# Attention and FFN layer: eight up tiles with one scale group's products in a PSUM bank of their own

## The chip, the cores and the metric

One core of one Trainium2 chip runs the kernel. The metric is the device time of one execution in microseconds. TensorE does the matrix products (PE in the profile), VectorE (DVE), ScalarE (ACT) and GpSimd (POOL) do the rest, and the SP queue issues the transfers.

## The reference

Sixteen sequences of 512 rows by 512 columns pass one transformer layer. The attention has 16 heads, low-rank queries and keys, ALiBi distances and a causal mask. The feed-forward part has 4-bit weights with one scale for each 128 inputs of an output row; that is the part which the change touches.

```python
x = x + _layernorm(attn(_layernorm(x), Wq_down, Wq_up, Wkv_down, k_up, v_up, Wo))
x = x + _layernorm(ffn(_layernorm(x), gate_up_packed, gate_up_scales, down_packed, down_scales))

def ffn(x, ...):                       # I = 1408, GROUP_SIZE = 128, H = 512: four groups of inputs
    w_gu = codes(gate_up_packed) * repeat(gate_up_scales.T, 128)      # [2816, 512]
    w_down = codes(down_packed) * repeat(down_scales.T, 128)          # [512, 1408]
    gate, up = split(x @ w_gu.T)
    y = (silu(gate) * up) @ w_down.T
    return y / sqrt(mean(y * y) + 1e-6)
```

## The kernel before, in words

The kernel works through 17 steps. Step t does the attention of sequence t and, beside it, the feed-forward part of sequence t - 1. Step 0 has attention alone, step 16 the feed-forward part alone, steps 1 to 15 have both. Every engine has its own written-out list of instructions, and semaphores tie the lists together; no scheduler moves anything.

**Precision.** fp32 values go through TensorE as a high and a low fp16 half, so one product of 128 inputs needs three matmuls of 128x512: high by high, high by low, low by high. A gate or up tile is 128 of the 1408 outputs for all 512 rows of a sequence. It sums four groups of inputs. The weights of such a tile are divided by the scale of the last group, so that the last group's weights are bare 4-bit codes, exact in fp16, and need two matmuls. That makes 3 x 4 - 1 = 11 matmuls (`GU_PRODUCTS`) for each of the 22 tiles (gate and up of m = 0 to 10). A down tile takes 33 matmuls, and there are four. Together 374 matmuls for each sequence.

**Slots.** The attention of a step is cut into 64 slots (`SLOTS`). Slots 0 to 22 compute the row maxima of two tiles each (`maximum` on TensorE, L1133 on VectorE, `row_sum` on ScalarE); slots 23 to 40 one such tile and one tile of exponentials; slots 41 to 63 two tiles of exponentials each. In slots 0 to 22 an even slot has tiles 128 and 256 wide in banks low0 and low1, an odd one 384 and 512 wide in score0 and score1. The exponentials of four heads are masked by GpSimd (`keep_causal(s)`, in the slot of e = 4s + 5) and multiplied into psO (`values(s)`, TensorE, in the slot of e = 4s + 7). After the maxima of its slot, TensorE runs a share of the 374 matmuls, from `cut(slot)` to `cut(slot + 1)`, by the weights in `PER_SLOT`; the first 22 run ahead of slot 0.

**The feed-forward jobs.** Job numbers run gate 0, up 0, gate 1, up 1 and so on, and take the three banks dense0 to dense2 in turn: a job may open only when the job three before it has been released (`open_job`). So up(m) opens when gate(m - 1) has been released, and gate(m + 2) when up(m) has. `up_done(m, up)` is the slot in which TensorE finishes the tile. One slot later ScalarE runs `tanh(m)`; two slots later VectorE runs `gate(m)` (L944), which releases the gate's bank. Two slots after the up tile is finished, VectorE runs `up(m)` (L952), which multiplies the bank into `tb` and releases it, and `h_high(m)` (L967); GpSimd follows with `h_low(m)` (L1260). All of these stand behind the maxima of their slot in the engine's list.

**The output rows.** Down tile i is copied by ScalarE (`y_copy(i)`, slot `down_done(i) + 1`), measured by VectorE (`y_moments(i)`, + 2), its root taken by GpSimd (`power(t, "lo", ...)`, L1190, + 3), normalised by VectorE (`y_norm(i)`, + 4) and added to the input by GpSimd (`y_add(i)`, L1266, + 5). The statistics of the next sequence (`ln1`) run on VectorE in slot 43 (`LN1_SLOT`, L828), their power on GpSimd in slot 45 (`LN1_POWER`) and the normalisation in slots 46 to 49. GpSimd's list decides: in slot 45 it waits first for the statistics of ln1, then for those of y 0, and only then does `keep_causal(6)`.

Of the kernel before, what the change touches and what calls it, by code (L numbers as in the profile page):

```python
# [65 lines left out]
LN1_SLOT, LN1_POWER, LN1_NORM = 43, 45, 46  # L66
# [20 lines left out]
LIFT = 8  # L87
D_PRODUCTS = 3 * MI
# [7 lines left out]
UP_PRODUCTS = 2 * MI * GU_PRODUCTS  # L96
# [24 lines left out]
def up_done(m, up):  # L121

    return done(GU_PRODUCTS * (2 * m + up + 1))
# [7 lines left out]
def layer_program(nc, x, wq_down, wq_up_t, wkv_down_t, k_up_t, v_up_t, wo_t, gu_packed, gu_scales,  # L131
# [6 lines left out]
    with ctx:  # L138
# [73 lines left out]
        h_scale = sb("h_scale", [P, MI], f32)  # L212
        st6 = {n: sb("st6_" + n, [P, NT, 6], f32) for n in ("ln1", "ln2", "ln3", "lo")}
# [19 lines left out]
        def st_bank(e):  # L233

            return score[e % 2] if e < THREE else (score + low_bank[1:])[e % 3]

# [122 lines left out]
        def _(pe):  # L359
# [49 lines left out]
            def step(t, att, ffn, nxt):  # L409
# [73 lines left out]
                def ffn_up(m, up, a, b):  # L483
# [5 lines left out]
                    tt = terms(lambda s, c: wgu[:, KC * s + c, col:col + P], lambda s, c: x2t[:, s, c, :], KC - 1)  # L489
                    tt += [(wgu[:, KC - 1, col:col + P], x2t[:, s, KC - 1, :]) for s in range(2)]  # L490
                    for c in range(KC if m == 0 and not up else 0):
# [3 lines left out]
                    if m or up:  # L495
                        ins = products(bank(t, n)[:, :], tt[a:b], a == 0, b == GU_PRODUCTS)
                    if b == GU_PRODUCTS:
                        ins.then_inc(sem["dense"], 1)
# [13 lines left out]
                def run(a, b):  # L512

                    start = 0
                    for q in range(2 * MI):
                        lo, hi = max(a, start), min(b, start + GU_PRODUCTS)
                        if lo < hi:
                            ffn_up(q // 2, q % 2, lo - start, hi - start)
                        start += GU_PRODUCTS
# [7 lines left out]
                def lse_rows(part):  # L527

                    dst = (psO, low_bank[0])[part]
                    pe.wait_ge(sem["mh"], val("mh", t, part + 1))  # L530
# [42 lines left out]
                def values(s):  # L573
# [3 lines left out]

                    pe.wait_ge(sem["keep"], val("keep", t, s + 1))
# [56 lines left out]
        def _(act):  # L635
# [15 lines left out]
            def step(t, att, ffn, nxt):  # L651
# [22 lines left out]

                def o_copy(g):
# [40 lines left out]
                if isinstance(t, int) and t == 1:  # L716
                    act.wait_ge(s_norm, 19)
# [45 lines left out]
                if ffn:  # L763
                    tanh(0)
                for slot, (low_tiles, exp_tiles) in enumerate(SLOTS):
# [17 lines left out]
                    if ffn:  # L783
                        for m in range(MI):
                            if m and slot == max(0, up_done(m, 0) + 1):
                                tanh(m)
                    for part in range(2):
# [20 lines left out]
        def _(dve):  # L808
# [103 lines left out]
            def step(t, att, ffn, nxt):  # L912
# [34 lines left out]
                def up(m):  # L947

                    n = job_f(t, m, 1)
                    dve.wait_ge(sem["dense"], val("dense", t, n + 1))  # L950
                    taken(dve, t, job_f(t, m, 0))
                    nc.vector.scalar_tensor_tensor(tb[:, m % 2, :], tb[:, m % 2, :], h_scale[:, m:m + 1],  # L952
                                                   bank(t, n)[:, :], ALU.mult, ALU.mult).then_inc(sem["freev"], 1)

                def h_high(m):

                    taken(dve, t, job_f(t, m, 1))
# [70 lines left out]
                def y_norm(i):  # L1028

                    dve.wait_ge(sem["rs"], val("rs", t, n_y[0] + i + 1))  # L1030
# [81 lines left out]
                n_y = [3 if nxt else 2]  # L1112
# [15 lines left out]
                for slot, (low_tiles, exp_tiles) in enumerate(SLOTS):  # L1128
# [31 lines left out]
                    if nxt and slot == LN1_SLOT:  # L1160
# [4 lines left out]
                        n_ln1 = n_ve[0]  # L1165
                    if nxt and LN1_NORM <= slot < LN1_NORM + NT:
                        i = slot - LN1_NORM
                        dve.wait_ge(sem["rs"], val("rs", t, n_ln1))
# [17 lines left out]
        def _(pool):  # L1186
# [20 lines left out]
            def divisors():  # L1207
# [3 lines left out]
                def put(ins, settle=True):  # L1211
                    n[0] += 1
                    ins.then_inc(s_norm, 1)
                    if settle:
# [24 lines left out]
                                            ALU.mult), False)  # L1239
                put(nc.gpsimd.tensor_scalar(gate_scale[:, :], divisor[:, 0:MI], 0.5 / (S_X * S_GU), None, ALU.mult))  # L1240
# [4 lines left out]
            def step(t, att, ffn, nxt):  # L1245
# [5 lines left out]
                n_y = (2 if ffn else 0) + (1 if nxt else 0)  # L1251
# [256 lines left out]
```

## Time and profile before

| | before |
|---|---|
| median of 3 runs | 2429.0 us (2428.91 to 2429.45) |
| profiled execution: time, span | 2428.72 us, 2427.0 us |
| TensorE matmul busy | 2349.2 us, 97% |
| VectorE busy | 1555.9 us, 64% |
| ScalarE busy | 1400.2 us, 58% |
| GpSimd busy | 669.0 us, 28% |
| mean granted TensorE clock | 0.987 |
| chain that ended last | PE 90%, DVE 5%, ACT 2% |

The chain names, for every stretch of time, the instruction that the end of the program waited on; PE 90% says that it runs through TensorE nearly all the time. A step with both parts repeats every 144.8 us. The step that is read below has slot 0 at 464.99 us, slot 23 at 509.1 us and slot 41 at 535.4 us; the one before it has slot 41 at 390.6 us.

### The profile page before, as it was taken

What the parts mean: (1) busy time and instruction counts of PE and PEld (TensorE: products, weight loads), DVE (VectorE), ACT (ScalarE), POOL (GpSimd) and SP (SyncE); (2) the same over time, 40 slices, a digit from 0 to 9 for tenths busy, and PEclk for the clock granted to TensorE, in tenths of its full rate; (3) what the DMA queues carried; (4) which work ended last, traced back from release to release, by engine and by line L of the source; (5) the groups of instructions that cost most, each with busy time, mean ns of one, the idle gap of its engine ahead of it and who ended that gap; (6) DMA issues with size and microseconds to landing.
All of it is one profiled execution on the core that took longest, in us unless ns stands there. A gap on an engine that the chain in (4) does not pass through costs nothing.

```text
span 2427.0 us, 38384 instructions
## 1 busy us (share of the span) xinstructions
PE 2349.2 (97%) x13020; PEld 1081.5 (45%) x13020; DVE 1555.9 (64%) x4344; ACT 1400.2 (58%) x3866; POOL 669.0 (28%) x923
## 2 busy tenths in 40 slices
PE   7699999999999999999999999999999999999988
PEld 3344444444444444444444444444444444444433
DVE  7867575665757666575765757566675765757542
ACT  4757466474656647466564755647475564756610
POOL 5522223132231312223132232312323132232312
PEclk8799999999999999999999999999999999999999
DMA  5020121202112120121202012120121202012000
GB/s 151 19 65 24 36 53 36 70 19 59 30 53 53 36 70 19 38 51 45 61 20 72 17 53 53 37 70 19 45 45 45 61 28 70 18 45 53 19 18 18
DMA packets 99523, 108.89 MB, mean 45 GB/s; under 512 B 22895, under 2 KB 73199, under 8 KB 99311
## 3 DMA queue, kind: packets, MB, share of 16 engines
q1 hardware_dynamic: 98462, 105.65, 16.5%
q8 instruction: 103, 1.69, 0.3%
q10 hardware_dynamic: 864, 0.79, 0.1%
q14 instruction: 94, 0.77, 0.1%
HBM read 38.49 MB, written 16.78 MB: 23 GB/s over the span
## 4 chain that ended last, share of the span: by engine, by line
PE 90%; DVE 5%; ACT 2%; issue 1%; POOL 1%; DMA 0%; SPq 0%; POOLq 0%; DVEq 0%; ACTq 0%
PE dense L379 65%; PE psO L583 6%; PE psO L379 4%; PE score L567 4%; PE low L550 3%; PE score L550 3%; DVE st_ln L828 1%; PE low L567 1%; ACT arena L770 1%; PE low L385 1%; PE low L474 1%; PE score L474 1%; PE score L385 1%; POOL arena L1323 0%; ACT score L687 0%
## 5 line engine op out<-in xcount | busy, mean ns | idle before, releaser
L379 PE MATMUL dense<-arena,wgu 128*128 128x512 f16 x3872 | 920.2, 379 | 1.5 <-DVE arena L931 1.2
L379 PEld LDWEIGHTS dense<-arena,wgu 128*128 128x128 f16 x3872 | 369.7, 97 | 394.0 <-issue 7.7
L379 PE MATMUL dense<-wdn,arena 128*128 128x512 f16 x2112 | 533.7, 379 | 2.6 <-POOL arena L1260 2.6
L1260 POOL TENSOR_TENSOR arena<-late,arena 128x512 f16<-128x512 f32 x176 | 203.4, 1155 | 821.6 <-DVE arena L967 611.9
L1133 DVE CUSTOM_DVE_ANT_0 low<-low,mmax 128x128 f32<-128x128 f32 (+3 forms) x672 | 278.9, 436 | 226.5 <-PE low L550 223.1
L770 ACT ACTIVATE arena<-score 128x512 f32<-128x512 f32 (+3 forms) x720 | 300.4, 437 | 173.6 <-PE score L567 131.2
L687 ACT ACTIVATE low<-low,ncol 128x128 f32<-128x128 f32 (+3 forms) x672 | 299.8, 446 | 121.9 <-DVE ncol L1133 114.7
L687 ACT ACTIVATE score<-score,ncol 128x384 f32<-128x384 f32 x352 | 214.3, 609 | 141.6 <-DVE ncol L1133 141.3
L379 PEld LDWEIGHTS dense<-wdn,arena 128*128 128x128 f16 x2112 | 198.7, 98 | 183.8 <-issue 9.3
L1133 DVE CUSTOM_DVE_ANT_0 score<-score,mmax 128x384 f32<-128x384 f32 x352 | 214.0, 649 | 75.1 <-PE score L550 74.6
L1323 POOL TENSOR_SCALAR_AFFINE_SELECT arena<-arena 128x512 f32<-128x512 f32 x240 | 162.3, 676 | 292.6 <-ACT arena L770 292.6
L567 PE MATMUL score<-qst,kst 128*128 128x512 f16 (+3 forms) x784 | 218.2, 305 | 2.7 <-ACT arena L770 2.5
L583 PE MATMUL psO<-arena 128*32 128x512 f32 (+3 forms) x1920 | 177.9, 443 | 24.1 <-POOL arena L1323 22.4
L972 DVE TENSOR_SCALAR arena<-oc 128x512 f16<-128x512 f32 x64 | 27.6, 431 | 224.6 <-ACT oc L681 222.1
L550 PE MATMUL low<-kst,qst 125*128 125x128 f16 (+3 forms) x672 | 155.5, 278 | 7.7 <-ACT low L687 7.4
L770 ACT ACTIVATE arena<-low 128x384 f32<-128x384 f32 (+3 forms) x240 | 103.5, 431 | 99.1 <-PE low L567 97.1
L672 ACT ACTIVATE late<-dense,gate_scale 128x512 f32<-128x512 f32 x176 | 119.6, 680 | 58.7 <-PE dense L379 38.3
L944 DVE SCALAR_TENSOR_TENSOR late<-late,dense 128x512 f32<-128x512 f32 x176 | 120.5, 685 | 51.4 <-ACT late L672 51.4
L952 DVE SCALAR_TENSOR_TENSOR late<-late,h_scale,dense 128x512 f32<-128x512 f32 x176 | 130.9, 744 | 24.7 <-PE dense L379 24.6
L1133 DVE DVE_READ_ACCUMULATOR2_ANT ncol<- 128x1 f32 x1024 | 145.3, 142 | 0.2
L1190 POOL TENSOR_TENSOR rs_ln<-ve_ln,half 128x4 f32<-128x4 f32 x48 | 49.3, 1026 | 328.2 <-DVE ve_ln L937 323.1
L687 ACT ACTIVATION_READ_ACCUMULATOR low<-low,ncol 128x1 f32 x672 | 132.1, 197 | 0.0
(181 smaller groups left out, 2917.5 us busy)
## 6 DMA issues: line engine op xcount, KB each, us to landing
qst<-arena SPq DMA_DIRECT2D x384, 64.0 KB, 2.0
kst<-arena SPq DMA_DIRECT2D x186, 128.0 KB, 2.6
xin<-x SPq DMA_DIRECT2D x16, 1024.0 KB, 5.1
late<-x SPq DMA_DIRECT2D x64, 256.0 KB, 2.8
out<-late SPq DMA_DIRECT2D x64, 256.0 KB, 2.0
qst<-mrow SPq DMA_DIRECT2D x96, 8.0 KB, 1.9
wgu<-wo_t SPq DMA_DIRECT2D x1, 1024.0 KB, 13.1
wgu<-wq_down SPq DMA_DIRECT2D x1, 768.0 KB, 4.4
```

The costliest lines, as they stand in the source:

```text
L379: ins = nc.tensor.matmul(dst, w, a, start=first and k == 0, stop=last and k == len(tt) - 1)
L550: nc.tensor.matmul(mx_bank(k)[:, 0:P * (i + 1)], qst[0:P - 3, h, P * i:P * i + P], kst[0:P - 3, h, 0:P * (i + 1)], start=True, stop=True). ...
L567: ins = nc.tensor.matmul(st_bank(e)[:, 0:wide], kst[:, h, P * kt:P * kt + P], qst[:, h, P * kt:L], start=True, stop=h >= STEEP)
L583: ins = nc.tensor.matmul(psO[HD * a:HD * a + HD, P * kt:L], v[:, kt, HD * (HG * g + a):HD * (HG * g + a) + HD], prob_of(s)[:, a, 0:wide], ...
L672: nc.scalar.activation(tb[:, m % 2, :], bank(t, n)[:, :], ACT.Tanh, scale=gate_scale[:, m:m + 1]).then_inc(sem["tanh"], 1)
L687: nc.scalar.activation(mx_bank(k)[:, 0:wide], mx_bank(k)[:, 0:wide], ACT.Exp, scale=-1.0, bias=ncol[:, k:k + 1], accum_out=scol[:, k:k + 1 ...
L770: nc.scalar.activation(prob_of(e // HG)[:, e % HG, 0:wide], st_bank(e)[:, 0:wide], ACT.Exp, scale=1.0 / S_SCORE).then_inc(sem["exp"], 1)
L944: nc.vector.scalar_tensor_tensor(tb[:, m % 2, :], tb[:, m % 2, :], 1.0, bank(t, n)[:, :], ALU.add, ALU.mult).then_inc(sem["freev"], 1)
L952: nc.vector.scalar_tensor_tensor(tb[:, m % 2, :], tb[:, m % 2, :], h_scale[:, m:m + 1], bank(t, n)[:, :], ALU.mult, ALU.mult).then_inc(sem ...
L1133: nc.vector.tensor_tensor_reduce(out=mx_bank(k)[:, 0:wide], in0=mx_bank(k)[:, 0:wide], in1=mmax[:, L - wide:L], scale=-1.0 / S_SCORE, scal ...
L1260: nc.gpsimd.tensor_tensor(ht[:, 1, m, :], tb[:, m % 2, :], ht[:, 0, m, :], ALU.subtract).then_inc(sem["hl"], 1)
L1323: nc.gpsimd.affine_select(out=diagonal, in_=diagonal, compare_op=ALU.is_ge, fill=0.0, base=0, pattern=[[0, HG], [1, P]], channel_multiplie ...
```

## The change

One more matmul can be saved in a tile if the third group (columns KC - 2) is also stored as bare codes: its product, two matmuls instead of three, then has another scale than the other groups and must be summed in a bank of its own. This is done for the up tiles m = 0, 1, 2, 3, 4, 5, 8, 9 (`BARE`), in steps 1 to 16. For these tiles:

- TensorE runs 8 matmuls into the main bank and 2 into psO (in step 16 into score0 or score1), 10 in place of 11. The first of the two waits for the previous copy out of psO (semaphore `bare`).
- ScalarE has a new instruction `bare_copy(m)`, one slot after the tile is finished: psO, times `bare_scale`, into the SBUF tile `own`.
- VectorE's `up(m)` becomes two instructions: an addition of the main bank and `own`, which releases the main bank and first waits for `bare`; then the multiplication by `tb`, from SBUF, which raises the new semaphore `whole`. `h_high(m)` waits for `whole`.

The sequence then has 366 matmuls, and `cut` deals these out over the same slots, so tiles begin and end at other places. The slots of `up_done(m, 0)` for m = 5, 6, 9, 10 go from 13, 16, 25, 30 to 12, 15, 24, 29, those of `up_done(m, 1)` for m = 7, 8, 10 from 20, 23, 32 to 19, 22, 31, and `down_done(1)` from 47 to 46. `LN1_SLOT`, `LN1_POWER` and `LN1_NORM` go from 43, 45, 46 to 45, 47, 48, with the counts of `rs` and `ve` to match. In step 0 GpSimd has three more small instructions.

```diff
-LN1_SLOT, LN1_POWER, LN1_NORM = 43, 45, 46
+LN1_SLOT, LN1_POWER, LN1_NORM = 45, 47, 48
...
+BARE = (0, 1, 2, 3, 4, 5, 8, 9)
+BARE_LOGS = 6
+def gu_products(q):
+    return GU_PRODUCTS - 1 if q % 2 and q // 2 in BARE else GU_PRODUCTS
...
+        def bare_bank(t, m):
+            return score[m % 2] if isinstance(t, int) and t == B else psO
...
+                    own_tt = [(wgu[:, KC - 2, col:col + P], x2t[:, s, KC - 2, :]) for s in range(2)] if bare else []
...
+                    if bare and b > last - n_own:
+                        first = max(a - (last - n_own), 0)
+                        if first == 0:
+                            k = BARE.index(m)
+                            if att and k == 0:
+                                taken(pe, t, j["V"] + 2)
+                            if att and k == BARE_LOGS:
+                                pe.wait_ge(sem["mrowc"], val("mrowc", t, 1))
+                            if k > (0 if att else 1):
+                                pe.wait_ge(sem["bare"], val("bare", t, k if att else k - 1))
+                        ins = products(bare_bank(t, m)[:, :], own_tt[first:b - (last - n_own)], first == 0, b == last)
...
+                def bare_copy(m):
+                    k = BARE.index(m)
+                    act.wait_ge(sem["dense"], val("dense", t, job_f(t, m, 1) + 1))
+                    if k:
+                        act.wait_ge(sem["whole"], val("whole", t, k))
+                    nc.scalar.activation(own[:, :], bare_bank(t, m)[:, :], ACT.Copy,
+                                         scale=bare_scale[:, m:m + 1]).then_inc(sem["bare"], 1)
...
+                            if m and m in BARE and slot == up_done(m, 1) + 1:
+                                bare_copy(m)
...
+                    values_ = bank(t, n)[:, :]
+                    if m in BARE:
+                        k = BARE.index(m) + 1
+                        dve.wait_ge(sem["bare"], val("bare", t, k))
+                        nc.vector.scalar_tensor_tensor(own[:, :], values_, 1.0, own[:, :], ALU.mult, ALU.add
+                                                       ).then_inc(sem["freev"], 1)
+                        taken(dve, t, job_f(t, m, 1))
+                        values_ = own[:, :]
                     taken(dve, t, job_f(t, m, 0))
                     nc.vector.scalar_tensor_tensor(tb[:, m % 2, :], tb[:, m % 2, :], h_scale[:, m:m + 1],
-                                                   bank(t, n)[:, :], ALU.mult, ALU.mult).then_inc(sem["freev"], 1)
+                                                   values_, ALU.mult, ALU.mult
+                                                   ).then_inc(sem["whole" if m in BARE else "freev"], 1)
```

Where the three engines stand now is shown by the order of their instructions. First VectorE in slots 4 and 5 of a step: the maxima (L1133, after L1205), `up(1)` and `h_high(1)`. Before:

```order
L1133 ISA low1,ncol<-low1,mmax 128x256 [waits s_mx]
L1133 ISA ncol 128x1
L952 SCALAR_TENSOR_TENSOR late<-late,h_scale,dense1 128x512 [waits s_freev,s_dense]
L967 TENSOR_SCALAR arena<-late 128x512 [waits s_freev]
L1133 ISA score0,ncol<-score0,mmax 128x384 [waits s_mx]
```

After:

```order
L1205 ISA low1,ncol<-low1,mmax 128x256 [waits s_mx]
L1205 ISA ncol 128x1
L1016 SCALAR_TENSOR_TENSOR own<-dense1,own 128x512 [waits s_bare,s_dense]
L1021 SCALAR_TENSOR_TENSOR late<-late,h_scale,own 128x512 [waits s_freev]
L1040 TENSOR_SCALAR arena<-late 128x512 [waits s_whole]
L1205 ISA score0,ncol<-score0,mmax 128x384 [waits s_mx]
```

The addition with its wait for ScalarE's copy stands between the maxima of slot 4 and those of slot 5.

TensorE in slot 7, where `up(3)` opens bank dense2, which `gate(2)` releases. Before:

```order
L550 MATMUL score0<-kst,qst 128x384 [waits s_rowsum]
L550 MATMUL score1<-kst,qst 128x512 [waits s_rowsum]
L379 MATMUL dense1<-arena,wgu 128x512 x3
L379 MATMUL dense2<-arena,wgu 128x512 [waits s_freev]
L379 MATMUL dense2<-arena,wgu 128x512 x3
```

After:

```order
L595 MATMUL score0<-kst,qst 128x384 [waits s_rowsum]
L595 MATMUL score1<-kst,qst 128x512 [waits s_rowsum]
L404 MATMUL dense1<-arena,wgu 128x512
L404 MATMUL dense2<-arena,wgu 128x512 [waits s_freev]
L404 MATMUL dense2<-arena,wgu 128x512 x5
```

The wait for the release has moved up by two matmuls within the slot. In the same way `gate(8)`, which opened as the second matmul of slot 20, now opens as the last of slot 19, while the up tile that it waits for is still read in VectorE's slot 19.

GpSimd in slots 36 to 50 (`keep_causal` is L1323 before and L1398 after; the group of four is 2 to 5). Before:

```order
L1323 AFFINE_SELECT arena<-arena 128x4x128 [waits s_exp] x4
L1190 TENSOR_TENSOR rs_ln<-ve_ln,half 128x4 [waits s_ve]
L1190 TENSOR_TENSOR rs_lo<-ve_lo,half 128x1 [waits s_ve]
L1323 AFFINE_SELECT arena<-arena 128x4x128 [waits s_exp]
L1266 TENSOR_TENSOR late<-late 128x512 [waits s_yn]
L1323 AFFINE_SELECT arena<-arena 128x4x128 [waits s_exp] x2
```

After:

```order
L1398 AFFINE_SELECT arena<-arena 128x4x128 [waits s_exp] x4
L1261 TENSOR_TENSOR rs_lo<-ve_lo,half 128x1 [waits s_ve]
L1398 AFFINE_SELECT arena<-arena 128x4x128 [waits s_exp]
L1261 TENSOR_TENSOR rs_ln<-ve_ln,half 128x4 [waits s_ve]
L1341 TENSOR_TENSOR late<-late 128x512 [waits s_yn]
L1398 AFFINE_SELECT arena<-arena 128x4x128 [waits s_exp]
```

The power of ln1 now stands behind `keep_causal(6)` instead of ahead of it. Further on `y_add(1)` (slot 51 in place of 52) has moved ahead of `keep_causal(9)`, which stands in slot 52.

## Rows read from the trace of the kernel before

**Rows 1.** The page: busy time, share of the span and instructions of each engine.

```profile
PE 2349.2 (97%) x13020; PEld 1081.5 (45%) x13020; DVE 1555.9 (64%) x4344; ACT 1400.2 (58%) x3866; POOL 669.0 (28%) x923
```

**Rows 2.** Stretches: busy us (instructions) of PE, PEld, DVE, ACT, POOL; slots 0-22, step.

```profile
464.99:509.10 44.11, 44.11 (x223) 21.02 (x222) 34.36 (x114) 31.05 (x102) 12.32 (x23) 1.00 0.12 27
...
428.10:573.00 144.90, 143.72 (x809) 65.89 (x806) 94.08 (x267) 86.79 (x241) 38.25 (x54) 1.00 0.17 45
```

**Rows 3.** Waits of PE: us in total, times, longest; the whole run, then one step.

```profile
PE psO L583 <- POOL arena L1323: 22.4, 16, 5.3
```

```profile
PE psO L583 <- POOL arena L1323: 1.2, 1, 1.2
```

**Rows 4.** Timeline of PE, slots 4 to 7 and 19: start, us, line, operation, tiles.

```profile
472.73 1.67 PE L379 MATMUL dense<-arena,wgu 128*128 128x512 f16 x7
474.24 0.54 PE L550 MATMUL score<-kst,qst 125*128 125x384 f16 x2
...
476.14 0.33 PE L550 MATMUL low<-kst,qst 125*128 125x128 f16 x2
...
478.03 0.54 PE L550 MATMUL score<-kst,qst 125*128 125x384 f16 x2
...
501.49 0.54 PE L550 MATMUL score<-kst,qst 125*128 125x384 f16 x2
```

**Rows 5.** Timeline of DVE: up(1), h_high(1), slot 5, gate(2), later up(6).

```profile
473.57 0.74 DVE L952 SCALAR_TENSOR_TENSOR late<-late,h_scale,dense 128x512 f32<-128x512 f32 x1
474.35 0.43 DVE L967 TENSOR_SCALAR arena<-late 128x512 f16<-128x512 f32 x1
474.76 0.57 DVE L1133 CUSTOM_DVE_ANT_0 score<-score,mmax 128x384 f32<-128x384 f32 x1
...
477.46 0.69 DVE L944 SCALAR_TENSOR_TENSOR late<-late,dense 128x512 f32<-128x512 f32 x1 [0.17 <-ACT late L672]
...
503.14 0.74 DVE L952 SCALAR_TENSOR_TENSOR late<-late,h_scale,dense 128x512 f32<-128x512 f32 x1
```

**Rows 6.** Timeline of ACT: last row sums of slots 3 and 5, then tanh(2).

```profile
472.28 0.66 ACT L687 ACTIVATE score<-score,ncol 128x512 f32<-128x512 f32 x1
...
476.07 0.66 ACT L687 ACTIVATE score<-score,ncol 128x512 f32<-128x512 f32 x1
...
476.75 0.68 ACT L672 ACTIVATE late<-dense,gate_scale 128x512 f32<-128x512 f32 x1
```

**Rows 7.** DVE timeline: a three-operand instruction from SBUF; ACT group: a plain copy from PSUM.

```profile
444.35 2.73 DVE L1055 SCALAR_TENSOR_TENSOR late<-arena,rs_ln,late 128x512 f32<-128x512 f32 x4
```

```profile
L708 ACT ACTIVATE late<-dense 128x512 f32<-128x512 f32 x64 | 39.4, 615 | 84.0 <-PE dense L379 84.0
```

**Rows 8.** Slots 43 to 52, one step earlier: timelines of DVE, POOL and PE.

```profile
396.67 2.47 DVE L828 BATCH_NORM_STATS2 st_ln<-xin 128x6 f32<-128x512 f32 x4
```

```profile
399.95 1.04 POOL L1190 TENSOR_TENSOR rs_ln<-ve_ln,half 128x4 f32<-128x4 f32 x1 [2.71 <-DVE ve_ln L937]
401.44 0.55 POOL L1190 TENSOR_TENSOR rs_lo<-ve_lo,half 128x1 f32<-128x1 f32 x1 [0.45 <-DVE ve_lo L1026]
...
403.27 1.50 POOL L1266 TENSOR_TENSOR late<-late 128x512 f32<-128x512 f32 x1 [0.68 <-DVE late L1035]
404.72 0.83 POOL L1323 TENSOR_SCALAR_AFFINE_SELECT arena<-arena 128x512 f32<-128x512 f32 x1
...
410.14 1.27 POOL L1266 TENSOR_TENSOR late<-late 128x512 f32<-128x512 f32 x1 [0.68 <-DVE late L1035]
411.37 0.63 POOL L1323 TENSOR_SCALAR_AFFINE_SELECT arena<-arena 128x512 f32<-128x512 f32 x1
```

```profile
402.64 0.64 PE L583 MATMUL psO<-arena 128*32 128x256 f32 x8 [1.18 <-POOL arena L1323]
...
405.69 0.43 PE L583 MATMUL psO<-arena 128*32 128x128 f32 x8
...
411.15 0.85 PE L583 MATMUL psO<-arena 128*32 128x384 f32 x8
```

More of the change, by code:

```diff
@@ L65, with norm_of_y, norm_of_x @@
 LN2 = 0.6931471805599453
-LN1_SLOT, LN1_POWER, LN1_NORM = 43, 45, 46
+LN1_SLOT, LN1_POWER, LN1_NORM = 45, 47, 48
+def norm_of_y(i, nxt):
+    return i + (4 if nxt and i else 3)
+def norm_of_x(ffn):
+    return 4 if ffn else 1
 BEHIND = 4
@@ L95 @@
 PER_SLOT[17], PER_SLOT[18], PER_SLOT[41] = 11, 10, 11
-UP_PRODUCTS = 2 * MI * GU_PRODUCTS
+UP_PRODUCTS = sum(gu_products(q) for q in range(2 * MI))
 ALL_PRODUCTS = UP_PRODUCTS + NT * D_PRODUCTS
@@ L121, in up_done @@
 def up_done(m, up):
-    return done(GU_PRODUCTS * (2 * m + up + 1))
+    return done(sum(gu_products(q) for q in range(2 * m + up + 1)))
 def down_done(i):
@@ L212, in layer_program @@
         h_scale = sb("h_scale", [P, MI], f32)
+        bare_scale = sb("bare_scale", [P, MI], f32)
+        own = sb("own", [P, L], f32)
         st6 = {n: sb("st6_" + n, [P, NT, 6], f32) for n in ("ln1", "ln2", "ln3", "lo")}
@@ L488, in ffn_up @@
                     col = I * up + P * m
-                    tt = terms(lambda s, c: wgu[:, KC * s + c, col:col + P], lambda s, c: x2t[:, s, c, :], KC - 1)
+                    last = gu_products(2 * m + up)
+                    bare = up and m in BARE
+                    tt = terms(lambda s, c: wgu[:, KC * s + c, col:col + P], lambda s, c: x2t[:, s, c, :],
+                               KC - 2 if bare else KC - 1)
                     tt += [(wgu[:, KC - 1, col:col + P], x2t[:, s, KC - 1, :]) for s in range(2)]
+                    own_tt = [(wgu[:, KC - 2, col:col + P], x2t[:, s, KC - 2, :]) for s in range(2)] if bare else []
+                    n_own = len(own_tt)
                     for c in range(KC if m == 0 and not up else 0):
@@ L529, in lse_rows @@
                     dst = (psO, low_bank[0])[part]
+                    if ffn and part == 0:
+                        pe.wait_ge(sem["bare"], val("bare", t, BARE_LOGS))
                     pe.wait_ge(sem["mh"], val("mh", t, part + 1))
@@ L576, in values @@
                     wide = L - P * kt
+                    if s == 0 and ffn:
+                        pe.wait_ge(sem["bare"], val("bare", t, len(BARE)))
                     pe.wait_ge(sem["keep"], val("keep", t, s + 1))
@@ L764, in step @@
                     tanh(0)
+                    bare_copy(0)
                 for slot, (low_tiles, exp_tiles) in enumerate(SLOTS):
@@ L1239, in divisors @@
                                             ALU.mult), False)
+                pool.wait_ge(s_norm, n[0])
+                put(nc.gpsimd.tensor_scalar(bare_scale[:, :], scales[:, MI:2 * MI, GROUPS - 2], 1 / (FP8_SCALE * S_GU), None,
+                                            ALU.mult))
+                for lo, hi in ((0, 6), (8, 10)):
+                    put(nc.gpsimd.memset(scales[:, MI + lo:MI + hi, GROUPS - 2], FP8_SCALE * S_GU), False)
                 put(nc.gpsimd.tensor_scalar(gate_scale[:, :], divisor[:, 0:MI], 0.5 / (S_X * S_GU), None, ALU.mult))
@@ L1329, in step @@
                     for i in range(NT):
-                        power(t, "lo", n_y + i + 1, i, i + 1)
+                        power(t, "lo", norm_of_y(i, nxt), i, i + 1)
                         y_add(i)
@@ L1344, in step @@
                     if nxt and slot == LN1_POWER:
-                        power(t, "ln1", n_y)
+                        power(t, "ln1", norm_of_x(ffn))
                     if isinstance(t, int) and t == 0:
```

36 lines of the change are left out of this document (19 added, 17 removed), and 2 rows, old and new, of the table COUNTS.

## The prediction, made before the changed kernel ran

> **What bounds the kernel now.** I read the page first, then the stretches, then the waits of TensorE. TensorE is busy for 97% of the span [rows 1], and in slots 0 to 22 of a step it has no gap at all: 44.11 us busy in 44.11 [rows 2]. In a whole step of 144.9 us it is idle for 1.2 us [rows 2, 3], at one place, `values(6)` in slot 47. So a matmul fewer is worth its own time, if nobody else is late next. Who could be late is the second thing to read. In slots 0 to 22 VectorE is busy for 34.4 of 44.1 us (78%) and ScalarE for 31.1 (70%) [rows 2], far more than their means of 64% and 58% [rows 1]. Six of the eight changed tiles lie there.
>
> **Matmuls removed.** Seven matmuls take 1.51 us (the first starts at 472.73, the next row-maximum at 474.24) [rows 4], 0.216 us each. A step with eight changed tiles saves 8 x 0.216 = 1.73 us of TensorE time, 16 steps save 27.6 us.
>
> **Work added.** VectorE: an addition of the form of `gate` (bank and SBUF, 0.69 us) and the multiplication, now from SBUF, at (2.73 - 0.69) / 3 = 0.68 us [rows 5, 7]. Between two dependent instructions there are 0.04 us (473.57 + 0.74, next at 474.35) [rows 5]. ScalarE: one copy with a pointer scale; the nearest rows are a plain copy at 0.615 and tanh, with a pointer scale, at 0.68 [rows 6, 7]. I take 0.66, near the tanh row. Its time alone lies beside TensorE's; its order does not.
>
> **What the order costs: a walk through one unit.** Slot 3, ScalarE: the last row sum starts at 472.28, and 0.68 later (as 476.07 to 476.75) the engine is free [rows 6], so `bare_copy(1)` runs from 472.96 to 473.62. Slot 4, VectorE: `up(1)`, which began at 473.57, now begins at 473.66 with the addition; 0.73 on comes the multiplication, 0.72 on `h_high`, and 0.41 on (474.35 to 474.76) slot 5's maxima: 475.52 instead of 474.76 [rows 5], 0.77 late. The row sums of slot 5, then tanh(2), then `gate(2)` each wait for the one before, so `gate(2)` ends at 477.46 + 0.69 + 0.77 = 478.92. TensorE opens `up(3)` behind that release. It used to do so after three matmuls of slot 7; now slot 7 starts 0.22 earlier (one matmul less in slots 0 to 6) and `up(3)` opens after one: 478.03 - 0.22 + 0.38 (an odd slot's two maxima) + 0.22 = 478.41. The release with 0.04 for the semaphore is at 478.96: TensorE **waits 0.55 us**.
>
> I carried the three lists on through slots 7 to 22 with durations read as start to start in the timelines of rows 4 to 6 (even slot: VectorE 0.60, ScalarE 0.38 + 0.47; odd slot: 1.13 and 0.64 + 0.68; gate 0.65, changed up tile 1.8 to 1.9, tanh and copy 0.57 and 0.55 until the next starts). With the old order they give the rows of slots 3 to 6 back to 0.02 us. One pass from the start of slot 5's maxima to those of slot 8's is 1.31 (to the second row maximum's value) + 0.68 + 0.72 (tanh) + 0.65 + 1.13 + 1.80 = 6.29 us, the next, through an even slot and `bare_copy`, 5.71; the mean is 6.0. TensorE needs for a unit of gate and up, 21 matmuls and 2.9 slots' maxima, 4.53 + 0.80 = 5.33. So the loop VectorE-ScalarE-VectorE becomes slower than TensorE for five units. In us from the start of slot 0, release against opening: up(3) 13.98 against 13.43, up(4) 19.53 against 19.23, up(5) 25.98 against 24.99. Waits: 0.55 + 0.30 + 0.99. The openings behind an addition, gate(3) to gate(7), come out with 0.5 to 1.1 us in hand, because it is the addition that releases.
>
> A fourth wait has nothing to do with lateness. `gate(8)` now opens as the last matmul of slot 19 and needs `up(6)`, which VectorE does in slot 19. Slot 19 started at 501.49 and `up(6)` was done at 503.14 + 0.74 = 503.88, 2.39 after the slot began [rows 4, 5]; TensorE gets there 0.38 + 6 x 0.216 = 1.68 after. Wait: 0.75. Sum of slots 0 to 22: **2.6 us a step**, for 15 steps. In slots 23 to 40 the same walk gives about 0.2 us, at row sums.
>
> The Trainium skill ("VectorE: DVE Perf Modes", section on the TRN2 errata) puts a ScalarE instruction from PSUM at 172 cycles plus one for each column, at 1.2 GHz; as an estimate that is 0.57 us for 512 columns. The rows have 0.615 for the plain copy [rows 7]. With 0.57 in place of 0.66 the three late releases would come about 0.1 us earlier each, and the total 4 us lower.
>
> **Slots 41 to 53.** Before, GpSimd takes the power of y 0 at 401.44, because VectorE does the four statistics of ln1 (from 396.67) first; `keep_causal(6)` stands behind it, and TensorE waits 1.18 us at 402.64 [rows 8]. With ln1 two slots later that wait goes, in 14 steps. What is late next: `keep_causal(7)` now stands behind ln1's power and `y_add(0)`. VectorE: y 0 from 396.9 for 1.49 (401.44 - 399.95), ln1 3.12 (from 396.75 to 399.87), so the power starts at 401.6 and takes 1.04, `y_add(0)` 1.27 to 1.50, `keep_causal(7)` 0.63 to 0.83 [rows 8]: done at 404.5 to 405.0. TensorE wants it at 405.69 - 1.18 - 0.22 = 404.29. Wait 0.2 to 0.7, I take 0.4. Then `y_add(1)` has moved ahead of `keep_causal(9)`. It starts at 410.14, tied to the copy after `values(7)`, and the mask behind it ran from 411.37 to 412.00; `values(9)` is wanted at 411.15 - 0.22 = 410.93 [rows 8]. Wait 1.1 us, in 15 steps, as the other sequence's statistics play no part in it.
>
> **The sum.** Steps 1 to 14: -1.73 - 1.18 + 2.6 + 0.2 + 0.4 + 1.1 = +1.4, x 14 = +19.5. Step 15, without ln1: -1.73 + 2.6 + 0.2 + 1.1 = +2.2. Step 16: the copy hides between tiles that are 4.5 us apart, -1.73. Step 0: its one wait of 5.3 us at the same `values` [rows 3] may go wholly or be replaced, 0 to -5.3; VectorE and GpSimd carry work on the weights there, I take -2. GpSimd's three small instructions run before TensorE wants the first tile: nothing. Together +18.0 on the profiled execution's 2428.7 us, which is 0.3 below the median: **2447 us**.
>
> **Rivals.** *Everything hides.* If the banks always come free in time, all 27.6 us and the 14 x 1.18 go, and step 0's 2: 2383 us. For it speak 97% on TensorE and 22% idle time of VectorE in the tight stretch; against it, that the idle time is spent waiting for row maxima and tanh, not free to be moved. The Trainium skill ("Perfetto Trace Analysis", section on the most-contended engine) has the engine of the highest occupancy optimised first; by that rule the result is this one. I give it 0.05. *Only the fixed waits stay (faster).* Place: the release of the banks by `gate(2)` to `gate(4)`. The point: the opening of `up(3)` has 478.41 - 478.19 = 0.22 us in hand without lateness; if the lateness handed on by a unit stays below that, the 1.84 us of late releases never arise. Then 2447 - 15 x 1.84 = 2419 us. It would need an addition and copy far shorter than every row of their form. Chance 0.13. *A part of them,* 2424 to 2434: 0.08. *More than forecast.* The row sums reach TensorE too late: a maximum in slot s + 2 needs slot s's sum, and in my walk several have only 0.1 us in hand; or the logs of the first half, which follow ScalarE's slot 16 through GpSimd into `lse_rows(0)` and a transfer, end up on the path. Up to 1 us more a step: 2462, up to 2470. Chance 0.12. *The forecast,* 2434 to 2460: 0.62. That the added work runs elsewhere than stated is excluded by the lists.
>
> **Range and chances.** The range leaves out the first rival and the far ends of the second and the last: 2412 to 2464. A measurement here can tell about 0.2% (5 us) from no change. Faster by more (below 2424): 0.19; within: 0.09; slower: 0.72.
>
> **What the profile after would show.** TensorE's waits for `freev` from L944's successor in slots 7, 10 and 13 and from `up(6)` in slot 19, once in each of 15 steps; a VectorE over 85% busy in slots 4 to 16; `values(6)` without a wait, `values(9)` with one of about 1.1 us on GpSimd. Fewer than 1 us of bank waits a step would prove the walk wrong, and waits of `lse_rows` on GpSimd would show the lateness elsewhere than I put it.

## The result, and the profile after

| | before | after |
|---|---|---|
| median | 2428.95 us (6 runs, 2428.42 to 2429.7) | 2450.11 us (6 runs, 2448.73 to 2451.44) |
| ratio | | 1.0087, 95% interval 1.0074 to 1.0100 |
| profiled execution: time, span | 2428.72, 2427.0 us | 2449.13, 2447.4 us |

The changed kernel is slower by 21 us (0.9%), though it runs 128 matmuls fewer. The forecast was 2447 us in 2412 to 2464, and slower. The page after, against [rows 1], and the head of the chain of work that ended last:

```profile
PE 2339.9 (96%) x12892; PEld 1061.6 (43%) x12892; DVE 1636.6 (67%) x4472; ACT 1452.9 (59%) x3994; POOL 666.4 (27%) x926
...
PE 73%; DVE 11%; ACT 7%; issue 5%; POOL 3%; DMA 1%; DVEq 0%; SPq 0%; POOLq 0%; ACTq 0%
```

TensorE's share of that chain was 90% and is 73%: VectorE and ScalarE are now on it for 18%, although their own busy shares rose by 3 and 1 points only. The stretches that answer to [rows 2], in the same columns (slots 4 to 16, slots 0 to 22, one step):

```profile
474.40:500.01 25.61, 24.28 (x121) 11.15 (x120) 22.19 (x70) 19.50 (x62) 4.84 (x5) 1.00 0.03 8
467.04:512.98 45.94, 43.99 (x219) 20.24 (x218) 38.68 (x121) 33.26 (x106) 13.12 (x24) 1.00 0.11 26
467.04:613.09 146.05, 142.97 (x799) 64.61 (x798) 98.95 (x275) 89.90 (x249) 38.04 (x54) 1.00 0.17 45
```

Slots 0 to 22 run four instructions fewer on TensorE than in [rows 2] and last 45.94 us instead of 44.11. In slots 4 to 16 VectorE is busy for 22.19 of 25.61 us, 87%. A step lasts 146.05 us; before it was 144.84 us. Both are read from the transposes of the log rows (the logarithms of the row sums), which TensorE runs once a step at the end of slot 19 in steps 1 to 15: first start to last start, divided by 14. First before, then after:

```profile
L531 PE MATMUL psO<-id,mh x15: 219/219/219, 214.0 to 2241.7; 128*96 128x128 f16 x15
```

```profile
L576 PE MATMUL psO<-id,mh x15: 219/219/220, 215.2 to 2259.9; 128*96 128x128 f16 x15
```

TensorE's waits in the whole run (us in total, times, longest), against [rows 3]:

```profile
PE psO L630 <- POOL arena L1398: 18.8, 19, 1.7
PE dense L404 <- DVE late L1005: 18.7, 30, 0.8
...
PE dense L404 <- DVE late L1021: 9.2, 15, 0.7
```

L1005 is `gate`, L1021 the multiplication of `up`, L1398 `keep_causal`. In the step whose slot 0 starts at 467.04, TensorE waits at four places, in this order: `up(3)` in slot 7, `up(5)` in slot 13, `gate(8)` in slot 19, and `values(9)`:

```profile
479.87 0.54 PE L595 MATMUL score<-kst,qst 125*128 125x384 f16 x2
481.08 1.47 PE L404 MATMUL dense<-arena,wgu 128*128 128x512 f16 x6 [0.45 <-DVE late L1005]
...
493.02 1.69 PE L404 MATMUL dense<-arena,wgu 128*128 128x512 f16 x7 [0.79 <-DVE late L1005]
...
507.14 0.39 PE L404 MATMUL dense<-arena,wgu 128*128 128x512 f16 x1 [0.61 <-DVE late L1021]
...
559.12 0.85 PE L630 MATMUL psO<-arena 128*32 128x384 f32 x8 [1.09 <-POOL arena L1398]
```

**How such a wait is to be read.** The matmul before a wait is drawn 0.38 us long, while the next could have started 0.216 us after it. So the wait printed is about 0.165 us too short, and one below that isn't printed at all. Better is the length of a slot, from the start of its first row maximum to that of the next slot's. An odd slot with seven matmuls lasts 1.89 us, an even one 1.68. All values are taken so from the timelines of the same step (us; "sum" is the start of slot 23 after that of slot 0):

| slot | opens | before | after | neither (4) | copy early (7) | cut shifted (9) | combined (10) |
|---|---|---|---|---|---|---|---|
| 2 | | 1.68 (7) | 1.90 (8) | 1.90 | 1.89 | 2.06 | 2.05 |
| 7 | up(3) | 1.89 | 2.52 | 1.89 | 2.13 | 2.30 | 1.92 |
| 10 | up(4) | 1.90 (8) | 2.16 | 2.02 | 2.16 | 2.17 | 2.17 |
| 13 | up(5) | 2.11 (8) | 2.86 | 1.91 | 2.16 | 2.63 (6) | 1.95 (6) |
| 19 | gate(8) | 2.16 (8) | 2.73 | 2.73 | 2.73 | 2.24 | 2.38 (9) |
| sum | | 44.13 | 45.94 | 44.20 | 44.85 | 45.45 | 44.00 |

(The heads of the last four columns give the number of the experiment. In brackets the matmuls where they aren't seven; slots 2 and 10 have eight in all columns from "after" on.) Slot 7 waits for 0.63 us, slot 10 for 0.26, slot 13 for 0.97, slot 19, which ends with the log rows, for 0.8.

The chain behind the wait in slot 7, against [rows 5, 6]: VectorE's `up(1)` as addition and multiplication, `h_high(1)`, the maxima of slot 5, `gate(2)`; then ScalarE's copy and tanh(2):

```profile
475.80 0.69 DVE L1016 SCALAR_TENSOR_TENSOR own<-dense,own 128x512 f32<-128x512 f32 x1 [0.24 <-ACT own L728]
476.52 0.75 DVE L1021 SCALAR_TENSOR_TENSOR late<-late,h_scale,own 128x512 f32<-128x512 f32 x1
477.31 0.43 DVE L1040 TENSOR_SCALAR arena<-late 128x512 f16<-128x512 f32 x1
477.65 0.56 DVE L1205 CUSTOM_DVE_ANT_0 score<-score,mmax 128x384 f32<-128x384 f32 x1
...
480.34 0.69 DVE L1005 SCALAR_TENSOR_TENSOR late<-late,dense 128x512 f32<-128x512 f32 x1 [0.79 <-ACT late L719]
```

```profile
475.01 0.68 ACT L728 ACTIVATE own<-psO,bare_scale 128x512 f32<-128x512 f32 x1
...
479.63 0.68 ACT L719 ACTIVATE late<-dense,gate_scale 128x512 f32<-128x512 f32 x1
```

The maxima of slot 5 start 10.61 us after slot 0, before it was 9.77 (474.76 - 464.99) [rows 5]. They are 0.84 us late (the walk had 0.77), tanh(2) and `gate(2)` with them.

On GpSimd `y_add(1)` (L1341) runs ahead of `keep_causal(9)`, the first of the two in the second row, and TensorE's `values(9)` at 559.12 starts when that is done; against [rows 8]:

```profile
556.80 1.50 POOL L1341 TENSOR_TENSOR late<-late 128x512 f32<-128x512 f32 x1 [2.65 <-DVE late L1108]
558.25 1.40 POOL L1398 TENSOR_SCALAR_AFFINE_SELECT arena<-arena 128x512 f32<-128x512 f32 x2
```

### The profile page after: what moved, and what is told of

Same layout as the page of the kernel before. It is cut to its first block, busy times and chain, and to the rows that moved or that the text cites. A ratio compares the mean times of both kernels' runs of the same rounds, so it can differ in the third digit from the quotient of the medians.

```text
span 2447.4 us, 38672 instructions
## 1 busy us (share of the span) xinstructions
PE 2339.9 (96%) x12892; PEld 1061.6 (43%) x12892; DVE 1636.6 (67%) x4472; ACT 1452.9 (59%) x3994; POOL 666.4 (27%) x926
## 4 chain that ended last, share of the span: by engine, by line
PE 73%; DVE 11%; ACT 7%; issue 5%; POOL 3%; DMA 1%; DVEq 0%; SPq 0%; POOLq 0%; ACTq 0%
PE dense L404 50%; PE psO L404 6%; PE psO L630 5%; PE score L612 4%; PE low L595 3%; ACT score L743 3%; DVE score L1205 2%; DVE late L1021 2%; POOL late L1341 1%; DVE own L1016 1%; ACT late L719 1%; PE score L595 1%; PE low L612 1%; ACT arena L829 1%; DVE st_ln L889 1%
## 5 line engine op out<-in xcount | busy, mean ns | idle before, releaser
L404 PE MATMUL dense<-arena,wgu 128*128 128x512 f16 x3488 | 863.1, 380 | 30.8 <-DVE late L1005 18.7
L404 PEld LDWEIGHTS dense<-arena,wgu 128*128 128x128 f16 x3488 | 330.3, 97 | 401.7 <-DVE late L1005 48.9
L1205 DVE CUSTOM_DVE_ANT_0 low<-low,mmax 128x128 f32<-128x128 f32 (+3 forms) x672 | 278.4, 438 | 124.8 <-PE low L595 122.9
L1398 POOL TENSOR_SCALAR_AFFINE_SELECT arena<-arena 128x512 f32<-128x512 f32 x240 | 158.7, 664 | 305.8 <-ACT arena L829 304.2
L1205 DVE CUSTOM_DVE_ANT_0 score<-score,mmax 128x384 f32<-128x384 f32 x352 | 212.8, 645 | 40.6 <-PE score L595 40.5
L1005 DVE SCALAR_TENSOR_TENSOR late<-late,dense 128x512 f32<-128x512 f32 x176 | 120.6, 685 | 75.8 <-ACT late L719 75.8
L1205 DVE DVE_READ_ACCUMULATOR2_ANT ncol<- 128x1 f32 x1024 | 143.8, 140 | 0.1
L1016 DVE SCALAR_TENSOR_TENSOR own<-dense,own 128x512 f32<-128x512 f32 x128 | 88.3, 690 | 65.1 <-ACT own L728 63.6
```

Source lines behind the costliest of these rows:

```text
L404: ins = nc.tensor.matmul(dst, w, a, start=first and k == 0, stop=last and k == len(tt) - 1)
L1016: nc.vector.scalar_tensor_tensor(own[:, :], values_, 1.0, own[:, :], ALU.mult, ALU.add).then_inc(sem["freev"], 1)
L1205: nc.vector.tensor_tensor_reduce(out=mx_bank(k)[:, 0:wide], in0=mx_bank(k)[:, 0:wide], in1=mmax[:, L - wide:L], scale=-1.0 / S_SCORE, scal ...
L1398: nc.gpsimd.affine_select(out=diagonal, in_=diagonal, compare_op=ALU.is_ge, fill=0.0, base=0, pattern=[[0, HG], [1, P]], channel_multiplie ...
```

## The experiments

Each time stands beside runs of the kernel before on the same chip. "A step" is the mean distance of the log rows, as above: 144.84 us before, 146.05 after.

**1. The move of ln1 alone, in the kernel before.**

```diff
-LN1_SLOT, LN1_POWER, LN1_NORM = 43, 45, 46
+LN1_SLOT, LN1_POWER, LN1_NORM = 45, 47, 48
```

> The kernel before with nothing but the statistics, power and normalisation of ln1 moved from slots 43, 45, 46 to 45, 47, 48. Theory: the wait of values(6) on GpSimd (1.2 us in 14 steps) goes and values(7) gets at most 0.1 us, as in the trace of the changed kernel, and step 0 gives 0.5 us: 2429 - 14 x 1.1 - 0.5 = 2413 us. Rival: GpSimd's list is as full as before and the wait only moves on to values(7) or values(8), so that the time stays at 2426 to 2429 us and the changed kernel owes nothing to this part.

Measured: 2414.93 us (4 runs), ratio 0.9941 (0.9926 to 0.9956); a step 143.88 us, 0.96 less. TensorE's wait for GpSimd at `values` is 5.4 us in the run instead of 22.4 [rows 3]:

```profile
PE psO L583 <- POOL arena L1323: 5.4, 16, 1.7
```

This part is a clear gain, hidden in the whole change by the others.

**2. gate(8) opened later.** Three matmuls go from slot 18 to slot 19, one from slot 19 to slot 20:

```diff
-    return F_FIRST + int(todo * sum(PER_SLOT[:slot]) / sum(PER_SLOT) + 0.5)
+    return F_FIRST + int(todo * sum(PER_SLOT[:slot]) / sum(PER_SLOT) + 0.5) + {19: -3, 20: -1}.get(slot, 0)
```

> The changed kernel with three matmuls moved from slot 18 to slot 19 and one from slot 19 to slot 20, so that gate(8) opens as the first matmul of slot 20 with nine before it in slot 19 instead of six. Theory of the fixed wait: up(6) releases the bank 2.4 us after slot 19 began, TensorE reaches the opening 0.38 + 9 x 0.216 + 0.38 = 2.7 us after it, so the wait of 0.6 to 0.77 us in 15 steps goes: 2450 - 11 = 2439 us. Rival: slot 19 now begins 0.65 us earlier and its maxima wait for the row sums of slot 17, so that the wait only changes its name: 2446 to 2450 us.

Measured: 2443.04 us (4 runs), ratio 1.0058 (1.0043 to 1.0073), 7 us less than after, not 11; a step 145.64 us. The wait for `up(6)` is gone. What waits next, neither theory had named: the log rows (L576) of slot 19 now start 0.14 us after the end of GpSimd's last step of the logs (L1392). TensorE first, then GpSimd:

```profile
504.27 2.11 PE L404 MATMUL dense<-arena,wgu 128*128 128x512 f16 x9
506.50 0.23 PE L576 MATMUL psO<-id,mh 128*96 128x128 f16 x1
```

```profile
506.11 0.25 POOL L1392 TENSOR_TENSOR mh<-lcol,mh 128x32 f16<-128x32 f32 x1
```

The ninth matmul starts 8 x 0.216 after 504.27, at 506.00, so the transpose could start at 506.21 and starts at 506.50: 0.29 us of the 0.77 came back as a wait, by these rows for the logs.

**3. y_add(1) behind keep_causal(9).**

```diff
-                            if slot == down_done(i) + 5:
+                            if slot == down_done(i) + (6 if i == 1 else 5):
                                 y_add(i)
```

> The changed kernel with y_add(1) one slot later on GpSimd, behind keep_causal(9) as before the change. Theory: values(9) loses its wait of 1.1 us in 15 steps: 2450 - 16.5 = 2433.5 us. Rival: the exponentials for keep_causal(9) come late as well, or the late addition of y 1 holds up the next output tile, and less than 5 us come back: 2445 to 2450 us.

Measured: 2433.02 us (10 runs), ratio 1.0014 (1.0005 to 1.0023), 17.1 us less than after; a step 144.90, 1.15 less. The order of two GpSimd instructions was worth 17 us.

**4. Neither copy nor addition.** ScalarE's `bare_copy` and VectorE's addition are left out, `up` multiplies the main bank. With them go TensorE's waits for the copy out of psO (`bare`), which these lines don't show:

```diff
-                            if m and m in BARE and slot == up_done(m, 1) + 1:
-                                bare_copy(m)
...
-                        nc.vector.scalar_tensor_tensor(own[:, :], values_, 1.0, own[:, :], ALU.mult, ALU.add
-                                                       ).then_inc(sem["freev"], 1)
-                        values_ = own[:, :]
```

> The changed kernel without the copy on ScalarE and without the addition on VectorE: up multiplies the main bank at once, as before the change, so that the third group's product never reaches the output; matmuls, their order and the cut are those of the changed kernel. Theory of lateness: the waits of up(3), up(4) and up(5) (0.61 + 0.27 + 0.95 us a step) go, those of gate(8) (0.7) and values(9) (1.1) stay: 2450 - 15 x 1.83 - 3 for slots 23 to 40 = 2420 us. Rival: the waits come from the cut, which opens up(3) to up(5) two or three matmuls earlier in their slots; then they stay and the time is 2440 us or more.

Measured: 2420.85 us (5 runs), ratio 0.9963 (0.9949 to 0.9977); a step 144.06. The slots in the table lose their waits but for 0.1 us in slot 10, gate(8) and values(9) keep theirs. So 1.99 us a step (146.05 - 144.06) come of the work that was added, and not of the cut alone; what the same work would cost on the cut of before was not run.

**5 and 6. One of the two alone.** First the copy without the addition; TensorE's waits for the copy stay here. Then the addition without the copy, with `tb` in place of `own` as its second input, so that nothing waits for a copy.

> The changed kernel with the copy on ScalarE but without the addition on VectorE: up multiplies the main bank at once, so that the third group's product never reaches the output. Theory: the copy fills time in which ScalarE waits for VectorE's maxima, and the lateness is made by VectorE; the time stays that of the run without both, 2421 us, at most 2424 us. Rival: the copy delays the row sums or tanh behind it and is the half of the loop that costs: 2435 us or more.

> The changed kernel with the addition on VectorE but without the copy on ScalarE: VectorE adds tb in place of the copied tile, the same form of instruction, so that the output is not the reference's. Theory: an addition that doesn't wait for the copy (0.24 to 0.55 us in the trace) starts earlier, but still puts 0.73 us in front of the next maxima in every unit; of the 1.83 us a step about half stays: 2421 + 14 = 2435 us. Rival 1: the whole loss is the addition's time: 2448 us. Rival 2: VectorE can hide the addition, the loss is its wait for ScalarE: 2421 us.

Measured: copy alone 2418.76 us (4 runs), ratio 0.9955 (0.9938 to 0.9971), a step 144.08; addition alone 2430.4 us (10 runs), ratio 1.0002 (0.9992 to 1.0011), a step 144.79. Against neither: copy +0.02 us, addition +0.73, both +1.99. The halves don't add up. (TensorE's waits for the copy cost nothing: run 5 has them and run 4 has not.) What is missing, 1.24 us a step, arises when VectorE's addition stands behind ScalarE's copy, which itself stands behind the row sums that VectorE's maxima release. I had expected a little more of the addition (2435).

**7. The copy one slot earlier.**

```diff
-                            if m and m in BARE and slot == up_done(m, 1) + 1:
+                            if m and m in BARE and slot == up_done(m, 1):
                                 bare_copy(m)
```

> The changed kernel with each bare copy (but the first) one slot earlier on ScalarE, behind the row sums of the slot in which TensorE finishes the tile. Nothing is left out. Theory: ScalarE is done with these row sums about when TensorE is done with the tile and waits for the next maxima, so the copy lies in a gap, and the addition doesn't wait any more: the same gain as leaving the copy out, 2450 - 14 = 2436 us. Rival: the copy waits for the tile and the row sums of the next slot start late, TensorE's maxima wait for them: 2448 us or more.

Measured: 2429.49 us (10 runs), ratio 1.0001 (0.9991 to 1.0010), 20.6 us less than after instead of 14; a step 144.78, that of the addition alone. In this trace slot 0 is at 464.64; the addition of `up(1)` doesn't wait and `gate(2)` ends 13.60 us after slot 0, against 13.99 after (480.34 + 0.69 - 467.04):

```profile
473.00 0.69 DVE L1016 SCALAR_TENSOR_TENSOR own<-dense,own 128x512 f32<-128x512 f32 x1
473.73 0.75 DVE L1021 SCALAR_TENSOR_TENSOR late<-late,h_scale,own 128x512 f32<-128x512 f32 x1
...
477.55 0.69 DVE L1005 SCALAR_TENSOR_TENSOR late<-late,dense 128x512 f32<-128x512 f32 x1 [0.79 <-ACT late L719]
```

So the lateness that comes of the copy is worth 1.27 us a step, 19 us in 15 steps, where I had put it at 0.93.

**8. Four changed tiles.** `BARE = (0, 5, 8, 9)`, with `y_add(1)` as in 3.

> The changed kernel with four tiles instead of eight (up 0, 5, 8, 9), which leaves 370 matmuls, and with y_add(1) behind keep_causal(9). Theory: a lone changed tile makes one release 0.77 us late; as the openings of slots 0 to 14 move by one matmul only, there is 0.65 us or more in hand and no bank wait is left, gate(8) opens in slot 20 again: kernel with ln1 moved alone, 2415 us, less 16 x 4 x 0.216 = 13.8 us: 2401 us, or 2405 us if the matmuls of step 16 again run at the lower clock at first. Rival: the lateness is there however few tiles there are, gate(7) to gate(9) wait for it: 2412 us or more.

Measured: 2418.29 us (4 runs), ratio 0.9955 (0.9940 to 0.9970), a step 144.13: a miss by 13 to 17 us. The time lies in the rival's range, though it is not gate(7) to gate(9) that wait. One wait of 0.8 us a step is left, at a place that the expectation passed over. With four tiles, as before the change, gate(6) is finished in slot 16, so VectorE does it in slot 18, and `up(7)` needs its bank in the same slot (TensorE, then VectorE):

```profile
497.88 0.82 PE L404 MATMUL dense<-arena,wgu 128*128 128x512 f16 x3 [0.63 <-DVE late L1005]
```

```profile
497.13 0.69 DVE L1005 SCALAR_TENSOR_TENSOR late<-late,dense 128x512 f32<-128x512 f32 x1 [0.36 <-ACT late L719]
```

Before the change slot 18 lasted 2.19 us with nine matmuls, 0.08 more than they need; here it lasts 2.91, since the maxima of slot 17 stand behind the addition of `up(5)` and start 0.85 us later in their slot (494.44 - 493.08 against 497.27 - 496.76). I had taken the room of slots 0 to 14 for that of all. Neither theory held as put: the lateness is not there everywhere, but a single tile ahead of the tightest opening is enough. (That place explains 0.8 x 15 = 12 us. A transfer of the log rows has a wait of 0.25 us in the same step and `values` one of 0.3 us in the step before; their part was not tried.)

**9. The cut one matmul later in slots 1 to 20, without 13 and 16, nothing else.**

> The changed kernel with only the cut one matmul later in slots 1 to 20 (but 13 and 16): each opening stands one matmul further behind the slot whose maxima lead to its release; gate(8) becomes the first matmul of slot 20. Theory of a slow loop: from slot 5 to slot 13 the waits are one lateness handed on, so that 0.22 us of room is a gain once a step, and gate(8) gains 0.3: 2450 - 15 x 0.5 = 2442 us. Rival, separate waits: each of the three loses 0.22 us, gate(8) 0.3: 2450 - 15 x 0.95 = 2436 us.

Measured: 2442.44 us (4 runs), ratio 1.0056 (1.0041 to 1.0071); a step 145.59, 0.46 less. In the table, slot 7 loses 0.22 us, slot 10 nothing, slot 13 has six matmuls now and still waits for 0.95. So the three waits are one lateness handed on, and room given at the head of the loop is a gain once.

**10. All together:** the copy early (7), `y_add(1)` (3), the cut one matmul later in slots 1 to 17 without 13, two in 18, three in 19, one in 20.

> All that the runs so far point to, nothing left out: eight changed tiles, the bare copies one slot earlier on ScalarE, y_add(1) behind keep_causal(9), and the cut one matmul later in slots 1 to 17 (two in slot 18, three in slot 19), so that up(3), up(4), up(5) open 0.22 us later against the slots that release them and gate(8) opens in slot 20. Theory: the run with early copies has 0.24, 0.14 and 0.25 us of such waits a step left, 0.77 at gate(8) and 1.1 at values(9); all but about 0.1 us go, and the log rows keep 0.2 us: 2429.5 - 16.5 - 15 x 1.1 = 2396 us. Rival: the lateness is handed on from unit to unit, so that 0.22 us of room helps once and not three times: 2403 us. Second rival: the slots that now begin earlier wait for row sums: 2410 us or more.

Measured: 2400.08 us (4 runs), ratio **0.9879** (0.9862 to 0.9895), 29 us less than before and 50 less than after; a step 142.81. The waits for `gate` (L1005) that the trace prints are 0.2 us in the whole run, once, instead of 18.7. By the table slot 7 waits for 0.03 us, slots 10 and 13 for 0.27 each, as much as with the early copy alone: the shift helped once, as the first rival has it. Slot 2 waits for 0.16 us, for row sums. The time lies between the theory and this rival; step 16 again began at the low clock (its first 19 matmuls took 6.33 us), which the 2396 left out.

**11 and 12. Both kernels profiled once more, unedited,** for the clock in step 16.

> A second profiled execution of the changed kernel, unedited, for one question: in step 16 the first 19 matmuls took 6.4 us at the lower clock and the 132 of the down tiles 30.3 us, against 4.3 and 28.7 us at the full clock in the kernel before. Theory: these 3.8 us belong to the execution, as the clock falls and rises at another moment in each; then at least one of the two stretches or their lengths differ here. Rival: they belong to the kernel; then both stretches take 6.4 and 30.3 us again.

> A second profiled execution of the kernel before, unedited, for the same question. Theory, clock of the execution: the first matmuls of step 16 or the 132 of the down tiles take longer here than in the first profile (52.4 us for the first 242, 28.65 us for the 132). Rival, clock of the kernel: 52.4 and 28.65 us again.

Step 16 in the first profiles: the first matmuls of `gate` and `up`, then the 132 of the down tiles, before and after:

```profile
2335.76 52.39 PE L379 MATMUL dense<-arena,wgu 128*128 128x512 f16 x242 [1.22 <-DVE arena L931]
2390.77 28.65 PE L379 MATMUL dense<-wdn,arena 128*128 128x512 f16 x132 [2.62 <-POOL arena L1260]
```

```profile
2354.09 6.37 PE L404 MATMUL dense<-arena,wgu 128*128 128x512 f16 x19 [0.95 <-DVE arena L992]
...
2409.48 30.34 PE L404 MATMUL dense<-wdn,arena 128*128 128x512 f16 x132 [2.62 <-POOL arena L1335]
```

The second profile of after (time 2449.13 us again, step 146.09):

```profile
2356.16 4.26 PE L404 MATMUL dense<-arena,wgu 128*128 128x512 f16 x19 [0.95 <-DVE arena L992]
```

The first stretch differs between executions of one program: 6.37 us once and 4.26 the other time. It was slow (5.9 to 6.6 us) in eight of the eleven profiles of kernels with changed tiles and in none of the three without, so whether the change makes it more likely stays open. What the second profile gained there it had lost in step 0 and the head of step 1, where the granted clock was 0.75 instead of 0.80 from 60 to 140 us and the log rows of step 1 came 1.6 us later. The second stretch took 30.34 us again, and in all eleven profiles of kernels with changed tiles 30.1 to 30.3; in the three of kernels without, 28.65 us each (the second profile of before gave 52.39 and 28.65 us again). The rows show the clock: in the changed kernel TensorE was idle for 2.62 us, then had 0.50 (1.2 GHz) in 2410 to 2412 (first two rows); before, after the same idle time, 1.00 (2.4 GHz) throughout (last two):

```profile
2409.00:2410.00 1.00, 0.52 (x2) 0.28 (x3) 0.00 (x0) 0.00 (x0) 0.33 (x1) 0.79 0.00 0
2410.00:2412.00 2.00, 2.00 (x6) 0.69 (x5) 0.00 (x0) 0.00 (x0) 0.00 (x0) 0.50 0.00 0
```

```profile
2391.00:2392.00 1.00, 1.00 (x6) 0.47 (x5) 0.00 (x0) 0.00 (x0) 0.00 (x0) 1.00 0.00 0
2392.00:2394.00 2.00, 2.00 (x11) 0.88 (x9) 0.00 (x0) 0.00 (x0) 0.00 (x0) 1.00 0.00 0
```

Why the clock drops at the same idle time in one kernel and not in the other stays open; the copy and the addition are not the reason, as the run with neither shows it too.

## Why the prediction was right, point by point

| us a step | forecast | measured | from |
|---|---|---|---|
| matmuls | -1.73 | -1.72 | step 16: 52.39 + 2.62 against 53.29 in run 7 |
| ln1: values(6), values(7) | -1.18 + 0.4 | -0.96 | run 1 |
| late releases, slots 23 to 40 | 1.84 + 0.2 | 1.99 | after - run 4 |
| gate(8) | 0.75 | 0.8 | slot 19 |
| values(9) | 1.1 | 1.15 | run 3 |
| sum | 1.4 | 1.26 (directly: 1.21) | log rows |

**The mechanism was right, and its sizes nearly so.** The walk had the releases at 13.98, 19.53 and 25.98 us from slot 0; in the trace gate(2), gate(3) and gate(4) end, with the 0.04 us for the semaphore, at 14.03, 19.54 and 25.97. So the three late banks, their order and the loop's 6.0 us a unit (5.51 and 6.43 between these ends) are confirmed. Experiments 4, 7 and 9 show the cause: without the added work the waits go, without VectorE's wait for the copy they shrink, and room helps once.

**Durations.** The copy took 0.68 to 0.70 us (0.66 was assumed, the plain copy has 0.615). By the Trainium skill ("VectorE: DVE Perf Modes", the TRN2 errata) the estimate was 0.57 us. The trace has 0.69 here and 0.615 for the plain copy, so the estimate doesn't hold. The multiplication from SBUF took 0.75 us, not 0.68. The prediction read 0.68 off the distance between the four starts in [rows 7]; each of the four is 0.745 us long by the groups of the trace. In these traces every such instruction (128x512, fp32 in and out) whose scale comes from a tile (a pointer) took 0.74 to 0.75 us, from bank or SBUF, and `gate` and the addition, with a constant, 0.69. The one from the bank at 0.74 [rows 5] was the nearer row. With it the walk's 0.77 us of lateness at slot 5 comes to the 0.84 that was measured.

**values(7)** was over-estimated: 0.1 us in the trace instead of 0.4. `keep_causal(7)` was done at 552.66 (552.02 + 0.64) and `values(7)` started at 552.72.

**The sum over the run** came out this near by luck, as misses cancel. From the first to the last log rows the change gave 17.0 us (forecast 14 x 1.4 = 19.5), step 15 with the rest 1.8 (2.2), step 0 -0.5 (-2), step 16 +2.1 (-1.73): 20.4 on the span, where 18.0 was forecast. In step 0 the 5.3 us wait of `values` did go, but smaller ones took its place (`values` 1.68 us, log rows 1.69 instead of 0.89); and this part, with the head of step 1, differs by 1.6 us between the two executions of the changed kernel. In step 16 the eight matmuls were saved (run 7: 53.29 us for what was 55.01), but the two stretches that had 1.2 GHz at first took 2.1 and 1.7 us more. That term failed: it counted the matmuls at full clock, with no bound for the clock though idle time stands before both stretches.

**The rivals.** *Everything hides* fell: TensorE's 97% said nothing on the slots in which the loop of VectorE and ScalarE decides, slots 4 to 16 or 25.6 us of a step. The Trainium skill ("Perfetto Trace Analysis", Identifying the Most-Contended Engine) has the engine with the highest occupancy optimised first; it forecasts no time, and the 2383 us are the prediction's reading of it. Here that engine's busy time fell by 9 us and the time rose by 21. *Only the fixed waits stay* had its price right: copy and addition left out gave 2421 us where 2419 was worked out. *More than forecast* did not come: in steps 1 to 15 of the trace of after no wait of the log rows for GpSimd is printed. They wait as soon as gate(8)'s wait is taken away (run 2), so the logs were the next thing late, behind that wait and not beside it.

## What to carry to other kernels

A busy share says what an engine does, not what it is waited for: before work is added to an engine with a third of its time free, follow the list of each engine through one unit and compare the period of the loop with that of the engine that bounds, since a lateness in a ring of banks is handed on. Where two engines alternate, the place of an instruction in its list can cost more than the instruction: the same copy one slot earlier gave 1.27 us a step back, one addition behind a mask 1.15 us. And take a bundle of edits apart, as the loss of one hides the gain of another: the move of ln1 was worth 14 us by itself, in the kernel before.

## What was not expected of the hardware

In step 16, after TensorE had been idle for 10.9 us, then busy with transposes, then idle for 0.95 us, the time until its clock is back at 2.4 GHz differs between executions of one program: the 19 matmuls there took 4.26 or 6.37 us. The Trainium skill ("TensorE: Matmul & The Clock Gate", Part 1) says of the start of a kernel that the number of slow matmuls varies from run to run; the two profiles of the changed kernel show the same in its last step. That the number varies does not explain the down tiles, 30.1 to 30.3 us in eleven profiles and 28.65 in three, after the same 2.62 us of idle time.
